# Moving the queries' cosine product of a rotary embedding from VectorE to GpSimd, with split sine buffers and semaphores

## What is computed

```
for i in range(6):
    x = attn_layer(shift_tokens(x), Wqkv[i], q_scale[i], k_scale[i], Wo[i]) + x
    x = ffn_layer(shift_tokens(x), ...) + x

def attn_layer(x, Wqkv, qs, ksc, Wo):            # 16 heads of 64
    q, k, v = split(x @ Wqkv)
    q = l2norm(q) * qs
    k = l2norm(k) * ksc
    q = q * cos * scale + rotate_half(q) * sin * scale
    k = k * cos / scale + rotate_half(k) * sin / scale
    return local_attention(q, k, v) @ Wo         # windows of 32, each sees itself and the one before
```

## Time and profile before

| what | us |
|---|---|
| median of 3 runs | 3242.11 |
| lowest and highest of them | 3240.98, 3242.28 |
| the profiled execution's own time | 3248.25 |
| its span in the profile | 3246.5 |
| granted TensorE clock, mean over the span | 0.959 of full speed |
| start of the first and the last of the 96 tiles' maxima (L1673) | 1416.4, 3183.7 |

### The profile page before, as it was taken

The page is one execution under the profiler, slowest core; times in us unless marked ns, Lnnn a source line. Parts: engine busy times, 40 slices in busy tenths (PEclk is TensorE's granted clock), DMA queues, the critical chain, the costliest instruction groups (busy, mean ns, idle before and its releaser), DMA issues. The chain is left out here.

```text
span 3246.5 us, 73988 instructions
## 1 busy us (share of the span) xinstructions
PE 2832.2 (87%) x29181; PEld 1570.2 (48%) x29181; DVE 2664.3 (82%) x4034; ACT 2148.6 (66%) x3298; POOL 1374.9 (42%) x819
## 2 busy tenths in 40 slices
PE   2999888888888879879988998998899889988998
PEld 1233233332333323346645764666376647655664
DVE  4999889888787778479978996998699879978995
ACT  2277777676655657767756775777577657756774
POOL 0200433425224210066635663666366536645661
PEclk8699999999988989989999999999999999999999
DMA  3200001010010120011111111111011111111110
GB/s 106 69 2 2 1 8 31 8 30 1 9 31 2 28 58 2 1 43 34 34 41 41 34 34 42 41 34 55 27 34 34 55 28 34 34 48 34 34 40 20
DMA packets 62987, 101.12 MB, mean 31 GB/s; under 512 B 20450, under 2 KB 45216, under 8 KB 61472
## 3 DMA queue, kind: packets, MB, share of 16 engines
q1 hardware_dynamic: 62636, 96.26, 10.9%
HBM read 38.30 MB, written 7.34 MB: 14 GB/s over the span
## 5 line engine op out<-in xcount | busy, mean ns | idle before, releaser
L916 DVE TENSOR_REDUCE a_part<-ps 128x1 f32<-128x512 f32 (+3 forms) x1664 | 987.2, 651 | 193.6 <-PE ps L594 185.9
L892 ACT ACTIVATE a_Pb<-ps 128x1024 f32<-128x1024 f32 (+3 forms) x832 | 762.8, 974 | 345.6 <-PE ps L763 343.4
L1273 PE MATMUL ps<-early 128*128 128x512 f32 x1152 | 563.4, 623 | 100.7 <-DVE l_qn L1651 76.4
L1210 POOL TENSOR_TENSOR l_sine<-l_qn,stack 128x512 f32<-128x512 f32 x192 | 345.1, 1797 | 254.0 <-DVE l_qn L1651 246.5
L1234 POOL TENSOR_TENSOR l_weights<-l_weights,l_rcp 128x1024 f32<-128x1024 f32 x96 | 182.5, 1901 | 485.5 <-DVE l_rcp L1688 485.5
L1273 PEld LDWEIGHTS ps<-early 128*128 128x128 f32 x1152 | 206.8, 193 | 330.4 <-issue 146.0
L594 PE MATMUL ps<-stack,a_QS 48*128 48x512 bf16 x1024 | 302.4, 406 | 73.3 <-DMA a_QS<-pieces 35.0
L1638 DVE TENSOR_REDUCE l_bounded<-l_square 128x8 f32<-128x512 f32 x384 | 252.2, 678 | 109.2 <-ACT l_square L1486 90.4
L1486 ACT ACTIVATE l_square<-ps 128x512 f32<-128x512 f32 x384 | 228.2, 597 | 129.6 <-PE ps L1273 128.7
L1659 DVE TENSOR_TENSOR l_cosine<-l_qn,stack 128x1024 f32<-128x1024 f32 x192 | 289.6, 1508 | 4.1
L644 PE MATMUL ps<-a_Pb,V 128*32 128x256 f32 (+1 forms) x3968 | 279.8, 399 | 0.0
(11 more groups left out here) (218 smaller groups left out, 5091.8 us busy)
## 6 DMA issues: line engine op xcount, KB each, us to landing
l_V_earlier<-l_V SPq DMA_DIRECT2D x96, 384.0 KB, 3.5
l_V_earlier<-l_V SPq DMA_DIRECT2D x96, 128.0 KB, 3.4
early<-in_L_ffn_Wqkv_dram SPq DMA_DIRECT2D x6, 1536.0 KB, 8.3
a_QS<-pieces SPq DMA_DIRECT2D x96, 64.0 KB
pieces<-a_piece SPq DMA_DIRECT2D x6, 512.0 KB, 2.6
pieces<-early SPq DMA_DIRECT2D x12, 256.0 KB, 2.7
a_KS<-pieces SPq DMA_DIRECT2D x48, 64.0 KB
l_w_o<-in_L_ffn_Wo_dram SPq DMA_DIRECT2D x6, 512.0 KB, 4.5
```

Source lines behind the costliest of these rows:

```text
L892: e.activation(Pb[:, n % 2, 2 * p:2 * p + 2, lo:CH], ps[:, 2 * p:2 * p + 2, lo:CH], ACT.Exp)\
L916: e.tensor_reduce(part[:, u % 2, column(h, qt), b:b + 1], bank[:, 0:width], AX.X, ALU.max)\
L1210: e.tensor_tensor(sine[:, :, 0:ROT], swap[:, :, ROT:LD], table[:, :, 0:ROT], ALU.mult).then_inc(s.rotated, 1)
L1273: e.matmul(ps[:, (V_BANK[T] if i == 2 else 0) + b, :], XS[:, T * P:(T + 1) * P], w_qkv[:, at:at + CH], start=True, stop=True).then_inc(s.v ...
```

## The change

For tiles 1 to 15 of each layer the queries' cosine product is written on POOL instead of DVE, and POOL's list is put in another order: the keys' sine product of tile T + 1 first, then the queries' cosine product of T + 1 and their sum, then the softmax weights of T, then the queries' sine product of T + 2. Tile 0 of a layer keeps its cosine product on DVE. `sine` becomes two buffers, and `rotated` becomes `sine_q`, `sine_k`, `hat_q` and `hat_k`; `cosine` counts keys alone and `cos_q` the queries.

```diff
-        sine = sb("sine", [P, LH, LD])
+        sine = sb("sine", [P, 2, LH, LD])
...
# gpsimd
-                def rotate(l, T, i):
-
-                    n = (l * NT + T) * 2 + i
-                    e.wait_ge(s.qn, 2 * n + 2)
+                def sines(l, T, i):
+
+                    n = l * NT + T
+                    e.wait_ge(s.qn, 4 * n + 2 * i + 2)
                     swap = qn[:, i, :, :]
                     table = tab[:, 2 * i + 1, T, :].unsqueeze(1).to_broadcast([P, LH, LD])
-                    e.wait_ge(s.rotated, START + n * 3)
-                    e.tensor_tensor(sine[:, :, 0:ROT], swap[:, :, ROT:LD], table[:, :, 0:ROT], ALU.mult).then_inc(s.rotated, 1)
-                    e.tensor_tensor(sine[:, :, ROT:LD], swap[:, :, 0:ROT], table[:, :, ROT:LD], ALU.mult).then_inc(s.rotated, 1)
-                    if i:
-                        return
-                    e.wait_ge(s.rotated, START + n * 3 + 2)
-                    e.wait_ge(s.cosine, START + n + 1)
-                    e.wait_ge(s.t_ready, START + (l * NT + T) * 4 - 2 if T else START + l * (4 * NT))
-                    e.tensor_tensor(by_head(hat[:, i, :]), cosine[:, i, :, :], sine[:, :, :], ALU.add).then_inc(s.rotated, 1)
+                    done = s.sine_k if i else s.sine_q
+                    e.wait_ge(s.hat_k if i else s.hat_q, START + n)
+                    e.tensor_tensor(sine[:, i, :, 0:ROT], swap[:, :, ROT:LD], table[:, :, 0:ROT], ALU.mult).then_inc(done, 1)
+                    e.tensor_tensor(sine[:, i, :, ROT:LD], swap[:, :, 0:ROT], table[:, :, ROT:LD], ALU.mult).then_inc(done, 1)
+
+                def cosines(l, T):
+                    n = l * NT + T
+                    e.wait_ge(s.hat_q, START + n)
+                    e.tensor_tensor(cosine[:, 0, :, :], qn[:, 0, :, :],
+                                    tab[:, 0, T, :].unsqueeze(1).to_broadcast([P, LH, LD]), ALU.mult).then_inc(s.cos_q, 1)
+
+                def add_queries(l, T):
+                    n = l * NT + T
+                    e.wait_ge(s.sine_q, START + 2 * n + 2)
+                    e.wait_ge(s.cos_q, START + n + 1)
+                    e.wait_ge(s.t_ready, START + n * 4 - 2 if T else START + l * (4 * NT))
+                    e.tensor_tensor(by_head(hat[:, 0, :]), cosine[:, 0, :, :], sine[:, 0, :, :], ALU.add).then_inc(s.hat_q, 1)
+
+                def first_tile(l):
+                    sines(l, 0, 0)
+                    add_queries(l, 0)
+                    sines(l, 0, 1)
...
                 def attend(l):
-                    rotate(l, 1, 0)
+                    sines(l, 1, 0)
                     for T in range(NT):
                         if T + 1 < NT:
-                            rotate(l, T + 1, 1)
+                            sines(l, T + 1, 1)
+                            cosines(l, T + 1)
+                            add_queries(l, T + 1)
                         normalise_weights(l, T)
                         if T + 2 < NT:
-                            rotate(l, T + 2, 0)
...
# tensor, turn
-                    e.wait_ge(s.rotated, START + (n * 2 + i) * 3 + 3)
+                    e.wait_ge(s.hat_k if i else s.hat_q, START + n + 1)
...
# vector, normalise
-                    if T:
-                        e.wait_ge(s.rotated, START + (n - 2) * 3 + (2 if i else 3))
-                    else:
-                        e.wait_ge(s.rotated, START + l * (6 * NT))
+                    e.wait_ge(s.sine_k if i else s.sine_q, START + 2 * (l * NT + T))
+                    if i == 0:
+                        e.wait_ge(s.cos_q, START + l * NT + T)
...
# vector, add_rotated
-                    n = (l * NT + T) * 2 + 1
-                    e.wait_ge(s.rotated, START + n * 3 + 2)
+                    n = l * NT + T
+                    e.wait_ge(s.sine_k, START + 2 * n + 2)
...
# vector, attend
                             normalise(l, 1, 0)
-                            cosines(l, 1, 0)
...
                             normalise(l, T + 2, 0)
-                            cosines(l, T + 2, 0)
```

More of the change, by code:

```diff
@@ L1088, in layers @@
     with ExitStack() as ctx:
-        s = semaphores(ctx, nc, "l_", "w_qkv w_tab w_o w_mlp xs tab a_ready v_ready square total root qn cosine v_done rotated "
+        s = semaphores(ctx, nc, "l_", "w_qkv w_tab w_o w_mlp xs tab a_ready v_ready square total root qn cosine v_done sine_q sine_k cos_q hat_q hat_k "
                        "t_ready t_free s_ready nmax sub exp_done sums rcp normed p_ready low high earlier_even earlier_odd "
@@ L1194, in _ @@
                 e.sem_inc(s.w_tab, 96)
-                e.sem_inc(s.rotated, START)
+                for signal in (s.sine_q, s.sine_k, s.cos_q, s.hat_q):
+                    e.sem_inc(signal, START)
                 e.memset(kT[:, 0, :, 0:WIN], 0.0).then_inc(s.clear, 1)
@@ L1219, in begin @@
+                def first_tile(l):
+                    sines(l, 0, 0)
+                    add_queries(l, 0)
+                    sines(l, 0, 1)
                 def begin(l):
                     e.wait_ge(s.w_tab, (l + 1) * 96)
-                    e.wait_ge(s.cosine, START + l * (2 * NT))
-                    e.wait_ge(s.rotated, START + l * (6 * NT))
+                    e.wait_ge(s.cosine, START + l * NT)
+                    e.wait_ge(s.cos_q, START + l * NT)
+                    e.wait_ge(s.sine_q, START + l * (2 * NT))
+                    e.wait_ge(s.sine_k, START + l * (2 * NT))
@@ L1227, in begin @@
                     e.wait_ge(s.tab, START + (l + 1) * 4)
-                    for i in range(2):
-                        rotate(l, 0, i)
+                    first_tile(l)
                 def normalise_weights(l, T):
@@ L1237, in attend @@
                 def attend(l):
-                    rotate(l, 1, 0)
+                    sines(l, 1, 0)
                     for T in range(NT):
                         if T + 1 < NT:
-                            rotate(l, T + 1, 1)
+                            sines(l, T + 1, 1)
+                            cosines(l, T + 1)
+                            add_queries(l, T + 1)
                         normalise_weights(l, T)
                         if T + 2 < NT:
-                            rotate(l, T + 2, 0)
-                for i in range(2):
-                    rotate(0, 0, i)
+                            sines(l, T + 2, 0)
+                first_tile(0)
                 with e.Fori(0, DEPTH - 1) as l:
@@ L1628, in _ @@
             def _(e):
-                for signal in (s.cosine, s.total, s.sub, s.added):
+                for signal in (s.cosine, s.total, s.sub, s.added, s.hat_k):
                     e.sem_inc(signal, START)
@@ L1656, in cosines @@
                     e.wait_ge(s.qn, 2 * n + 2)
-                    if T == 0 and i == 0:
+                    if T == 0:
                         e.wait_ge(s.tab, START + (l + 1) * 4)
+                    if i == 0:
+                        e.wait_ge(s.hat_q, START + l * NT)
                     e.tensor_tensor(cosine[:, i, :, :], qn[:, i, :, :],
-                                    tab[:, 2 * i, T, :].unsqueeze(1).to_broadcast([P, LH, LD]), ALU.mult).then_inc(s.cosine, 1)
+                                    tab[:, 2 * i, T, :].unsqueeze(1).to_broadcast([P, LH, LD]), ALU.mult)\
+                        .then_inc(s.cosine if i else s.cos_q, 1)
                 def add_rotated(l, T):
-                    n = (l * NT + T) * 2 + 1
-                    e.wait_ge(s.rotated, START + n * 3 + 2)
+                    n = l * NT + T
+                    e.wait_ge(s.sine_k, START + 2 * n + 2)
                     e.wait_ge(s.cosine, START + n + 1)
                     e.wait_ge(s.t_ready, START + (l * NT + T) * 4 if T else START + l * (4 * NT))
-                    e.tensor_tensor(by_head(hat[:, 1, :]), cosine[:, 1, :, :], sine[:, :, :], ALU.add).then_inc(s.rotated, 1)
+                    e.tensor_tensor(by_head(hat[:, 1, :]), cosine[:, 1, :, :], sine[:, 1, :, :], ALU.add).then_inc(s.hat_k, 1)
                 def maxima(l, T):
```

## The result

The changed kernel takes 3481.56 us (median of 4 runs, 3464.81 to 3489.52) against 3242.2 us before on the same chip: a ratio of 1.072 (95% interval 1.070 to 1.075), slower. The profiled execution after is 3481.48 us, 233.2 us over that of before. Runs of one kernel differ by up to 1.1%, and the traces show one reason: the layers' first maxima start between 1404 and 1421 us in the traces of this study, although nothing ahead of the layers differs.

A forecast was written before the change was run, and what follows sets the result against it. A ring through each tile, not DVE's load alone, was taken as the bound at 15.44 us; at 18.0 us a tile, 40.4 us a layer and 242 us in six gave 3484 us, range 3390 to 3600.

The forecast's parts named there:

- The ring through POOL: Keys' scaling, POOL's sines, cosine and queries' sum (7.64 us), PE's turn, next keys' scaling: 17.04 us a tile without collision.
- The price of POOL's product: The queries' cosine product on POOL was to take 2.36 us, like the table product of the same shape.
- The collision: DVE's keys' cosine and POOL's operations wait for each other: 17.91 us a tile with POOL first, 18.16 with DVE first.
- The clock: Rival: PE's pauses lower its granted clock in the loop, 3565 to 3637 us, from 3520 if in some tiles; chance 0.26.
- The sum: Per layer +33.1 us for thirteen intervals, +3.7 for the first, +3.6 for the last: 40.4, 242 us in six.
- PE's pause: Sign: PE idles 3 us or more ahead of the queries' turn, released by POOL's sum.
- The interval of 17.9 to 18.2 us: Sign: DVE's maxima (L1673) follow each other every 17.9 to 18.2 us in the loop.
- the order of POOL's rows: Sign: POOL runs sine, sine, cosine, sum without pauses from the keys' scaling on.
- DVE's long cosine row: Sign: DVE's keys' cosine or sum spans over 1.8 us, or has a pause ahead.
- what leaves DVE: One queries' cosine product a tile, 1.87 us on DVE, of which only 0.51 us was to be gained on the ring.
- prompt sums: DVE summing the keys' squares sooner after the second square: 0.51 us a tile, 15.44 to 14.93 us.
- the rival of 3199 us: POOL's chain stays hidden and 0.51 us is won over 14 tiles in six layers, 43 us; chance 0.03.

The follow-up runs named there:

- the old order: The changed kernel with the queries' cosine product kept on POOL, but directly behind the queries' sine product and ahead of the keys' sine: 3282.0 us, ratio 1.010.

## Why the prediction held, and where it did not

*The ring through POOL* held, part by part. From the keys' scaling to the queries' sum: 7.41 us (1517.33 to 1524.74) where 7.64 was forecast; POOL's issue took 0.08 instead of 0.17 and its gap 0.16 instead of 0.24. From the end of the sum to the queries' scaling 3.78 (3.91), to the key projection 0.74 (0.70), to the next keys' scaling 5.61 (5.66). Together 17.54, forecast 17.91. That it is this ring was shown by taking half the product away (1.08 us a tile) and by moving it one place (2 us a tile).

*The price of POOL's product*: 2.37 us, forecast 2.36 from the table product.

*The collision* held: 3.27 us for 1.22, and 1.21 with one operand. Which came first was left open; POOL's sum did, by 0.16 us (1522.40 against 1522.56), in nearly all tiles. In a layer's last interval DVE came first, as forecast, and the two took turns, with POOL's cosine at 3.33 us and its sum at 3.12. Timeline of DVE, then of POOL, in the first layer's last interval:

```profile
1662.95 1.26 DVE L1676 TENSOR_TENSOR l_cosine<-l_qn,stack 128x1024 f32<-128x1024 f32 x1
1664.35 3.16 DVE L1685 TENSOR_TENSOR l_hat<-l_cosine,l_sine 128x1024 f32<-128x1024 f32 x1
```
```profile
1663.09 3.33 POOL L1218 TENSOR_TENSOR l_cosine<-l_qn,stack 128x1024 f32<-128x1024 f32 x1
1666.58 3.12 POOL L1226 TENSOR_TENSOR l_hat<-l_cosine,l_sine 128x1024 f32<-128x1024 f32 x1 [0.16 <-POOL l_cosine L1218]
```

*The clock* was kept as a rival, with a chance of 0.26: PE's pauses were to bring what stands behind that of 5.36 us at the start of the second layer, a granted clock of 0.50 and four matmuls of 3.62 us that take 1.98: 3565 to 3637 us if in all tiles, from 3520 if in some. The low clock is a part of the sum instead: a third of the inner tiles, 0.7 us each, where 0.9 was priced for POOL coming first. It also lengthened the first and the last intervals, in all six layers: the granted clock is 0.81 to 0.90 in the first ones and 0.82 to 0.91 in the last, which take 18.0 to 19.2 us where 17.3 was forecast, +4.9 us on average instead of +3.6.

*The sum*, and the luck in it: forecast 242 us, measured 237: 22.9, 185.2 and 29.2 us, where 22, 199 and 22 were forecast. Two misses stand against each other. At full clock the first interval takes 17.0 us, the inner 17.53 and the last some 16.65 (from the run with PE kept busy), where 18.0, 18.0 and 17.3 were forecast: by an estimate from these some 197 us in all, 45 less than forecast. The rest, some 40 us, goes with the low clock, which the sum had left out: a sixth of the loss.

*PE's pause* was taken at 3.3 to 4.4 us, from the end of PE's last projection at 4.5 us after the keys' scaling to the turn at 7.8 to 8.9, and is 2.10, so one of the signs named (3 us or more) did not come. It was reckoned from a row of six matmuls of 2.84 us, where the view stopped short: PE runs eight of them there, 3.70 us, before as after (1519.08), so its last projection ends 0.9 us later than was taken. Timeline of PE before, over a longer window:

```profile
1509.42 3.70 PE L1273 MATMUL ps<-early 128*128 128x512 f32 x8
```

The interval of 17.9 to 18.2 us was another sign that failed, since the mean of 17.82 is made of 17.5 and 18.25; the order of POOL's rows, DVE's long cosine row and its lower busy share came as named.

*Wrong: what leaves DVE.* The step that gave "prompt sums" 0.51 us a tile on the ring of the kernel before does not hold. The walk from the queries' scaling to the keys' scaling, in which DVE was late, is not part of the ring that set the tile before; PE has work ahead of the query projection until later than the keys' scaling in any case (1.19 us later). Cutting the product to a sixteenth left the tile at 15.44 us, and the two runs with it whole in another place of POOL's list have 15.48 and 15.60. So taking it off DVE was worth nothing in the loop, and the rival of 3199 us, built on the 0.51, had no ground. The forecast used the 0.51 too, but on another ring: its 5.66 us from the key projection to the keys' scaling are 6.17 as before less 0.51, and there the step held, for the new ring does run over the keys' sums, which now wait for their square, and the term measured 5.61. The expectation for the old order took the 0.51 as a gain and missed by 0.1 to 0.7 us a tile.

## What to carry to other kernels

An engine that is busy for 92% of a tile need not be the bound: follow the ring from an instruction back to itself one tile later, and count only what stands on it; an instruction beside it can be cut without a gain, as this cosine product, whose row shrank from 1.87 to 0.87 us for nothing in the loop. When work is handed to an engine with room, its place in that engine's in-order list decides: behind what it must wait for, and ahead of whom. Here the same instruction in the same list cost 2.1 us a tile in one place and 0.04 in the next.

## What the runs showed of the hardware

GpSimd's product of 128x1024 with a broadcast table takes 2.37 us, nearly twice VectorE's 1.22; half of it (128x512) takes 1.27 us, and with it the tile lost 1.08 us. A VectorE reduction over an axis of one element moves 128x1024 in 1.21 us beside a GpSimd instruction that reads SBUF, where a product with two SBUF operands took 3.27 us, some 2 us more than alone. And the granted clock fell to 0.50 for 3.4 us behind a pause of TensorE of only 2.08 us, and to 0.91 over the tile in a third of the tiles, though a tile at 1.00 had an equal pause (2.10 us); it stayed at 1.00 between a layer's tiles 1 and 14 with pauses of 1.0 us (half the product), and with six small matmuls of 1.14 us in the pause in all inner tiles but one.
